# A four-layer graph network on one core: attention scores from 32-row matmuls, one head per row group and PSUM bank

## What is computed

```
h = relu(layernorm(x))                                   # [128, 128, 256]
q, k, v = split(h @ w_qkv)                               # 8 heads of 32
attn = einsum('bhnd,bhmd->bhnm', q, k) * 32 ** -0.5
attn = softmax(where(adj == 0, -inf, attn))
o = einsum('bhnm,bhmd->bhnd', attn, v) @ w_proj + b_proj
x = x + o + layernorm(o) * gamma + beta
# then three more layers: scores normalised by their norm; a graph attention
# with leaky ReLU and softmax; adj @ x @ weight + bias
```

## Time and profile before

| what | before |
|---|---|
| device time, median of 3 runs | 1971.55 us (1969.12 to 1973.96) |
| span of the profiled execution | 1971.0 us, 0.55 us under that median |
| PE busy | 1831.1 us, 93% |
| weight loads (PEld) busy | 1602.2 us, 81% |
| DVE busy | 1609.3 us, 82% |
| ACT busy | 1084.3 us, 55% |
| POOL busy | 674.6 us, 34% |
| chain that ended last, by engine | PE 48%, DVE 25%, issue 15%, POOL 9%, ACT 3% |

### The profile page before, as it was taken

The page is one execution under the profiler, slowest core; times in us unless marked ns, Lnnn a source line. Parts: engine busy times, 40 slices in busy tenths (PEclk is TensorE's granted clock), DMA queues, the critical chain, the costliest instruction groups (busy, mean ns, idle before and its releaser), DMA issues.

```text
span 1971.0 us, 39957 instructions
## 1 busy us (share of the span) xinstructions
PE 1831.1 (93%) x13064; PEld 1602.2 (81%) x13064; DVE 1609.3 (82%) x4485; ACT 1084.3 (55%) x2756; POOL 674.6 (34%) x1045
## 2 busy tenths in 40 slices
PE   6899999999999999999999999999999999999974
PEld 5788888878878888888878878788888878878864
DVE  3688897888888887887888888888887988978874
ACT  3555565655655555655655655655655655655632
POOL 3233333333333333333333333333332333333331
PEclk8999999999999999999999999999999999999987
DMA  2000000000000000000000000000000000000000
GB/s 88 12 17 17 23 23 11 21 16 16 21 17 16 22 16 17 21 16 16 22 16 16 21 17 16 22 16 16 22 16 16 22 16 16 21 16 17 12 6 17
DMA packets 37975, 37.85 MB, mean 19 GB/s; under 512 B 2416, under 2 KB 37488, under 8 KB 37872
## 3 DMA queue, kind: packets, MB, share of 16 engines
q1 hardware_dynamic: 37872, 36.84, 5.7%
HBM read 20.05 MB, written 16.78 MB: 19 GB/s over the span
## 4 chain that ended last, share of the span: by engine, by line
PE 48%; DVE 25%; issue 15%; POOL 9%; ACT 3%; DVEq 0%; POOLq 0%; DMA 0%; ACTq 0%
PE bank L314 15%; PE mid L387 11%; DVE stats L683 6%; DVE x L764 5%; PE bank L322 4%; POOL o_res L909 4%; POOL rstd L899 4%; PE bank L507 3%; PE mid L370 3%; PE bank L512 3%; PE bank L487 3%; DVE x L849 3%; DVE h_t_lo L699 2%; DVE o_gam L756 2%; ACT h_t_hi L559 2%
## 5 line engine op out<-in xcount | busy, mean ns | idle before, releaser
L567 ACT ACTIVATE probs<-mid,neg_max 128x128 f32<-128x128 f32 x1024 | 284.8, 379 | 105.2 <-DVE neg_max L713 105.2
L379 PE MATMUL mid<-k_diag,q_t 128*128 128x512 f32 x512 | 273.6, 617 | 0.0
L559 ACT ACTIVATE h_t_hi<-bank 128x512 fp32r<-128x512 f32 x192 | 114.9, 599 | 251.7 <-PE bank L322 251.6
L387 PEld LDWEIGHTS mid<-v,probs_t 128*128 128x128 f32 x2048 | 244.3, 192 | 3.3
L387 PE MATMUL mid<-v,probs_t 128*128 128x33 f32 x2048 | 239.9, 272 | 0.0
L899 POOL TENSOR_TENSOR rstd<-var_eps,minus_half 128x2 f32<-128x2 f32 x320 | 226.4, 707 | 25.1
L693 DVE TENSOR_SCALAR z<-x,mean_var,rstd 128x256 f32<-128x256 f32 x384 | 205.2, 575 | 10.8 <-POOL rstd L899 3.2
L713 DVE TENSOR_REDUCE neg_max<-mid 128x8 f32<-128x1024 f32 x128 | 154.6, 1208 | 51.1 <-issue 38.0
L897 POOL TENSOR_TENSOR var_eps<-mean_var,eps 128x2 f32<-128x2 f32 x320 | 66.0, 206 | 363.9 <-DVE mean_var L687 363.9
L322 PEld LDWEIGHTS bank<-ident,z 128*128 128x128 f32 x768 | 94.8, 152 | 112.4 <-DVE z L693 73.1
L322 PE MATMUL bank<-ident,z 128*128 128x128 f32 x768 | 125.8, 288 | 61.3 <-DVE z L693 61.3
(11 more groups left out here) (133 smaller groups left out, 5485.0 us busy)
## 6 DMA issues: line engine op xcount, KB each, us to landing
x<-in_x SPq DMA_DIRECT2D x64, 256.0 KB, 2.6
out_x<-x SPq DMA_DIRECT2D x64, 256.0 KB, 2.2
w_qkv_sb<-in_w_qkv SPq DMA_DIRECT2D x1, 768.0 KB, 4.8
w_q_sb<-in_w_q SPq DMA_DIRECT2D x1, 256.0 KB, 5.0
w_k_sb<-in_w_k SPq DMA_DIRECT2D x1, 256.0 KB, 5.3
w_proj_sb<-in_w_proj SPq DMA_DIRECT2D x1, 256.0 KB, 5.2
w_v_sb<-in_w_v_t SPq DMA_DIRECT2D x1, 256.0 KB, 5.4
w_gat_sb<-in_w_gat SPq DMA_DIRECT2D x1, 256.0 KB, 5.7
```

What stands on the lines that cost most here:

```text
L379: last = pe.matmul(mid[:, s], q_t[:, par, hc, b * N:(b + 1) * N], k_diag[:, hc, :, b * N:(b + 1) * N], start=False, stop=True)
L387: last = pe.matmul(mid[:, b, h * W33:(h + 1) * W33], probs_t[:, b * HC + h // RG, h % RG], v0[:, par, b, h], start=True, stop=True)
L559: act.activation(h_t[k][0][:], bank[:], ACT.Relu).then_inc(h_hi_ready[k], 1)
L567: last = act.activation(probs[:, s, r], mid[:, s, r * N:(r + 1) * N], ACT.Exp, bias=neg_max[:, s, r:r + 1])
```

## The change

The four heads of a chunk lie in q and k as projected in four groups of 32 rows. After the change each of the 16 blocks is a matmul of its own over 32 rows and 128 columns, with `tile_position=(r * 32, 0)`, so that it uses one row group of the array; the heads of row group r go to bank r of `mid`. `k_diag` becomes `k_t`, which one ACT copy of `bank6` fills; `keys_apart` is gone, on ACT and on DVE, and so is the fill of `k_diag` with zeros. `neg_max`, `probs` and `probs_t` are laid out by row group first. Both graphs' scores are made together, after q, the output projection and v, when all four banks are free. The order on ACT and DVE changes with that. A cut of the diff:

```diff
-        k_diag = sb("k_diag", [128, HC, RG, 2 * N])
+        k_t = sb("k_t", [128, HC, 2 * N])
...
@@ PE
-                def scores(b):
-
-                    for hc in range(HC):
-                        s = b * HC + hc
-                        pe.matmul(mid[:, s], ident_b[:], mask_b[:].unsqueeze(1).to_broadcast([128, RG, N]),
+                def scores():
+
                     for r in range(RG):
+                        pe.matmul(mid[:, r], ident_b[:], mask_b[:].unsqueeze(1).to_broadcast([128, BC, N]),
                                   start=True, stop=False)
-                        last = pe.matmul(mid[:, s], q_t[:, par, hc, b * N:(b + 1) * N],
-                                         k_diag[:, hc, :, b * N:(b + 1) * N], start=False, stop=True)
+                    for b in range(2):
+                        for hc in range(HC):
+                            s = b * HC + hc
+                            for r in range(RG):
+                                at = slice(r * HD, (r + 1) * HD)
+                                last = pe.matmul(mid[:, r, s * N:(s + 1) * N], q_t[at, par, hc, b * N:(b + 1) * N],
+                                                 k_t[at, hc, b * N:(b + 1) * N], start=False, stop=s == BC - 1,
+                                                 tile_position=(r * HD, 0))
                     last.then_inc(scores_psum, 1)
...
-                if middle:
-                    pe.wait_ge(q_ready, done(p2))
-                    pe.wait_ge(k_ready[0], done(p2))
-                    pe.wait_ge(k_ready[1], done(p2))
-                    wait_before(pe, o_heads_ready, p2, 2)
-                    scores(0)
...
                 if middle:
+                    pe.wait_ge(q_ready, done(p2))
+                    pe.wait_ge(k_ready, done(p2))
+                    wait_before(pe, o_heads_ready, p2, 2)
                     wait_before(pe, o_lo_ready, p2)
                     wait_before(pe, o_ready, p2)
-                    scores(1)
+                    scores()
...
-                if middle:
-                    transpose_probs(0)
...
-                if middle:
-                    transpose_probs(1)
                 if gat:
                     pe.wait_ge(h_hi_ready[2], done(p4))
                     pe.wait_ge(h_lo_ready[2], done(p4))
                     rows(bank4, h_t[2], w_gat_p, 0, hw_psum)
+                if middle:
+                    transpose_probs(0)
                 if front:
                     pe.wait_ge(v0_ready, done(p1))
                     columns(bank6, w_qkv_p, D, h_t[0], k_psum)
+                if middle:
+                    transpose_probs(1)
...
@@ ACT
                 if front:
-                    keys_apart(act, p1, 0)
+                    act.wait_ge(k_psum, done(p1))
+                    act.activation(k_t[:], bank6[:], ACT.Copy).then_inc(k_ready, 1)
...
@@ DVE
-                if middle:
-                    maxima(0)
                 if relation:
                     dve.wait_ge(o_psum, done(p3))
...
                     normalize(2, p4, z[2], x2[:, par], z_ready[2])
+                if middle:
+                    maxima(0)
...
                 if gat:
                     relu_lo(2, p4, bank4)
+                if middle:
+                    maxima(1)
                 if relation:
                     dve.wait_ge(x1_ready, done(p3, 2))
                     moments(1, p3, x1[:, 1 - par])
-                if middle:
-                    maxima(1)
...
-                if front:
-                    keys_apart(dve, p1, 1)
```

More of the change, by code:

```diff
@@ L184, in gnn_stack @@
         q_psum, k_psum, v0_psum = sem("q_psum"), sem("k_psum"), sem("v0_psum")
-        q_ready, k_ready, v0_ready = sem("q_ready"), [sem(f"k_ready{i}") for i in range(2)], sem("v0_ready")
+        q_ready, k_ready, v0_ready = sem("q_ready"), sem("k_ready"), sem("v0_ready")
         scores_psum, max_ready = sem("scores_psum"), sem("max_ready")
@@ L261, in gnn_stack @@
         SPLIT = [(w_proj_sb, w_proj_p), (w_v_sb, w_v_p), (w_gat_sb, w_gat_p), (w_out_sb, w_out_p)]
[L264 to L271, removed]
         @block.sync
@@ L381, in scores @@
                     last.then_inc(scores_psum, 1)
                 def heads_times_values(b):
-                    pe.wait_ge(probs_t_ready, done(p2, BC) - HC * (1 - b))
+                    if b == 0:
+                        pe.wait_ge(probs_t_ready, done(p2, RG))
                     for h in range(H):
-                        last = pe.matmul(mid[:, b, h * W33:(h + 1) * W33], probs_t[:, b * HC + h // RG, h % RG],
+                        last = pe.matmul(mid[:, b, h * W33:(h + 1) * W33], probs_t[:, h % RG, b * HC + h // RG],
@@ L559, in relu_hi, with exps, copy_probs_t @@
                     act.activation(h_t[k][0][:], bank[:], ACT.Relu).then_inc(h_hi_ready[k], 1)
[L561 to L568, removed]
+                def exps(r):
+                    if r % 2 == 0:
+                        act.wait_ge(max_ready, done(p2, 2) - (1 - r // 2))
+                    wait_before(act, probs_t_psum, p2, RG)
+                    for s in range(BC):
+                        last = act.activation(probs[:, r, s], mid[:, r, s * N:(s + 1) * N], ACT.Exp,
+                                              bias=neg_max[:, r, s:s + 1])
                     last.then_inc(probs_ready, 1)
-                def copy_probs_t(s):
-                    act.wait_ge(probs_t_psum, done(p2, BC) - (BC - 1 - s))
+                def copy_probs_t(r):
+                    act.wait_ge(probs_t_psum, done(p2, RG) - (RG - 1 - r))
                     wait_before(act, heads_psum, p2, 2)
-                    act.activation(probs_t[:, s], mid[:, s], ACT.Copy).then_inc(probs_t_ready, 1)
+                    act.activation(probs_t[:, r].rearrange("p s m -> p (s m)"), mid[:, r], ACT.Copy)\
+                       .then_inc(probs_t_ready, 1)
                 if front:
@@ L578, in step @@
                     act.activation(q_t[:, 1 - par], bank6[:], ACT.Copy, scale=SCALE).then_inc(q_ready, 1)
-                if middle:
-                    exps(0)
-                if middle:
-                    exps(1)
+                if front:
+                    act.wait_ge(v0_psum, done(p1))
+                    act.activation(v0[:, 1 - par, :, :, 0:HD], bank6[:].rearrange("p (b h d) -> p b h d", b=2, h=H),
+                                   ACT.Copy).then_inc(v0_ready, 1)
                 if last_layer:
@@ L591, in step @@
                     relu_hi(2, p4, bank4, [hw_psum])
-                if front:
-                    act.wait_ge(v0_psum, done(p1))
-                    act.activation(v0[:, 1 - par, :, :, 0:HD], bank6[:].rearrange("p (b h d) -> p b h d", b=2, h=H),
-                                   ACT.Copy).then_inc(v0_ready, 1)
+                if middle:
+                    exps(0)
                 if last_layer:
@@ L600, in step @@
                 if middle:
+                    exps(1)
+                if gat:
+                    act.wait_ge(hw_psum, done(p4))
+                    act.activation(hw[:], bank4[:], ACT.Copy).then_inc(hw_ready, 1)
+                if middle:
                     copy_probs_t(0)
@@ L603, in step @@
                     copy_probs_t(1)
-                if gat:
-                    act.wait_ge(hw_psum, done(p4))
-                    act.activation(hw[:], bank4[:], ACT.Copy).then_inc(hw_ready, 1)
                 if middle:
```

39 lines of the change are left out of this document (18 added, 21 removed).

## The result

The changed kernel takes 2228.64 us, median of four runs (2220.48 to 2236.22), against 1971.87 for the kernel before, also four runs: 1.1299 times as long, interval 1.1273 to 1.1324. That is 257 us more, where 112 were forecast. The sign is right, but the size is more than double. The time lies inside the range of 2025 to 2232 by luck: its upper end was set by the rival with a shared weight path, at 2228 us, and the trace refutes that rival. That both say 2228 is chance.

What follows compares the result with a forecast made beforehand. A step was taken as PE's 13.04 us plus 15.80 us set by DVE. 45 steps at 2.19 us and 14 loop turns at 0.94 us add 112 us to 1971.0: 2083 us, range 2025 to 2232.

Steps and rivals of the forecast that it cites:

- shared weight path: Rival for the score blocks on PE: row groups' weight loads do not overlap, S = 3.56 us; 257 us more, 2228 us; 12%.
- Which stretch bounds: Per step, PE's 13.04 us plus 15.80 us set by DVE; scores lie in DVE's stretch, so PE time saved there gains nothing.
- The walk of one step: Following one full step in the new order to `y_t_lo`: 1.09 us + S later, 2.19 us more with S = 1.1.
- S: Time from first to last start of the 16 score blocks on PE; taken as 1.1 us, row groups side by side.
- The estimate of 1.16 us: Alternative figure for the score blocks' first-to-last start time on PE: 3.56 us divided by the skill's measured 3.07x.
- The turn of the loop: At each of 14 hardware-loop turns DVE's 3.00 us stall covers the projection wait, so a turn costs 0.94 us more.
- PE is long done with v at a turn: At a loop turn, PE finishes v before DVE's stall ends, so masks can start once `o` is read, at 1024.95.
- The clock: Rival: PE's new idle gaps drop its granted clock to half for 4.32 us of products; at most 254 us more, 2330 us; 6%.
- Half overlap: Rival for the score blocks on PE: pairs side by side or issue-limited, S = 1.78 us; 152 us more, 2123 us; 13%.
- hidden S: Rival: the score blocks' time on PE hides behind DVE's work; 60 us more, 2031 us; 8%.
- PE as the bound: Rival: PE limits after all, so shorter scores save 2.34 us in 64 steps, 150 us off, 1822 us; 7%.
- The collision of `x3b`: Rival: POOL's `x3b` add no longer meets DVE's z(1), 1.54 us becoming near 0.8; 45 us off 2083, 2038 us; 4%.

Runs made afterwards that it cites:

- two_steps: The changed kernel with a hardware loop of 2 steps in place of 4, no fillers; four runs took 2135.33 to 2215.53 us, no ratio given.
- before_padded: The kernel before with 24 one-column matmuls, read by nobody, added per step where PE waits for z(1); 2003.69 us, ratio 1.0158.
- before_two_steps: The kernel before with a hardware loop of 2 steps in place of 4; 1937.54 us, ratio 0.9824.
- filler_two_steps: The changed kernel with 17 unread filler matmuls a step in PE's gaps and a hardware loop of 2 steps in place of 4; 2066.01 us, ratio 1.0475.
- experiment 4: The kernel before, keeping full-height scores and keys copied apart, with the changed kernel's order on PE, ACT and DVE; 2253.43 us, ratio 1.1407.
- filler: The changed kernel with 17 unread matmuls a step in PE's two gaps, loop of 4 steps; 2146.19 us, ratio 1.0877.
- experiment 3: The changed kernel with its 16 score blocks issued row group by row group, so neighbours share rows and bank; 2384.61 us, ratio 1.2091.
- own_bank: The changed kernel with a 2-step loop, six fillers, projection in bank 5 ahead of q, scores before v, DVE and ACT reordered; 1920.76 us, ratio 0.9734.

## Why the prediction was right or wrong

**The 257 us, by differences of medians.** The order: 2066.01 - 1937.54 = 128.5. The turns of the loop: (2146.19 - 2066.01) - (1971.87 - 1937.54) = 45.9. The clock: 2228.64 - 2146.19 = 82.4. These are paths through four kernels, so they close by construction, and another path would share out the sum otherwise: with the short body the clock costs 69 us in the quickest run of `two_steps`, and more in the others. What each contains is shown apart: the order's by steps of 30.95 against 28.85 us, 31 of the 45.9 by `before_padded`, the clock's by the granted clock. Some 10 of the other 15 us are no long body's: `before_two_steps` pays 0.4 us in every second step, which `filler_two_steps` does not. The last 5 are open: the fillers lengthen the body once more (q8 153 packets), and what that costs was not tried.

**Which stretch bounds: right.** The scores lie in DVE's stretch, and the time saved on them on PE came to nothing. DVE's and ACT's key copies were worth nothing either: DVE lost 137 us of work, but PE's stretch, from `y_t_lo` to the next `x2`, is 14.9 us at full clock and was 15.0.

**The walk of one step: right.** Forecast 2.19 us, found 2.17 in a step at full clock. Its terms: `o` 0.82 us after DVE is ready, forecast 0.8; 0.97 for the scores, forecast 1; 1.23 for POOL, forecast 1.2; the `x1` pair 0.88, forecast 0.90. S, from first to last start, was 0.90 us, forecast 1.1. What S lacks stands around it: ahead of the blocks the four masks take 0.97 us (995.59 to 996.56) instead of 0.88, and the maxima start 0.43 us behind the last block's start instead of 0.35. The three misses cancel, so part of the agreement is luck.

By the Trainium skill, "TensorEngine Tiling (Array Packing)", Key Properties, tiles load and multiply in parallel; this trace agrees, with 0.90 us against 2.55 group by group. The same section of the Trainium skill says that a change of the tiling mode drains TensorE; the 0.09 us more ahead of the blocks may be that, and nothing here tells it from other causes. The estimate of 1.16 us from the Trainium skill's "TensorE: Matmul & The Clock Gate" was too high: the 0.90 us are a quarter of 3.56, as four groups side by side would have it.

The 128.5 us of experiments 6 and 7 look like 59 steps at 2.17. In their traces a step costs 2.1 us more, and the stretch from the first `y_t_lo` to the last 114 us; the other 15 come ahead of the first `y_t_lo`, at 130.6 us instead of 115.6, where no cost was forecast.

**The turn of the loop: failed.** "PE is long done with v at a turn" was the step. PE with 24 more pairs in a step has a fetch stall of its own (3.87 us), q comes late by it, and DVE then waits 5.39 us for PE. That a stall of DVE can cover the wait for the projection was right in kind: in experiment 4 no turn is dearer. But DVE's stall was no fixed cost of the turn; it was a fetch too, gone in a body half as long. The turns were forecast at 0.94 us more each, 13 us in all. Measured where the clock is up, the 13 steps with a turn take 37.2 us on average in `filler` and 32.3 in the kernel before: 4.9 us more each, 63 us, of which the order would account for 2.1 each. (The body runs 14 times, with 13 jumps back.)

**The clock: failed, and the larger miss.** The sum has no term for the clock, because "a gap of 2.23 us at a turn left the granted clock at 1.00". That was read from one turn and taken as a rule. The trace of the kernel before has 13 such turns, with gaps of 2.0 to 2.4 us on PE, and behind 8 of them the granted clock fell. The very next one, with a gap of 2.08 us at 1144.50:

```profile
1144.00:1151.00 7.00, 6.50 (x30) 4.42 (x31) 6.04 (x17) 4.81 (x14) 3.58 (x4) 0.76 0.11 37
```

The turn steps with a fall take 32.3 to 32.9 us, those without 31.7 to 31.8. So the evidence lay in the trace of the kernel before, and gaps of this kind, 1.76 and 2.36 us, now came twice in every step. The mechanism stood among the rivals at 6%, with up to 254 us (2083 and 254 make 2337, not 2330); 82 were found. The loss has a second part, that the rival did not have: in a step at the low clock the exponentials come late too (the ACT rows in the chain above), and PE's own stretch is up to 16.3 us instead of 14.9.

**The rivals.** Shared weight path: refuted by S = 0.90 us and by experiment 3, though its number was met. Half overlap and hidden S: refuted by the 0.90 us and by the wait of 0.97. PE as the bound: refuted, DVE's three waits decide. It comes true in the layout of `own_bank`, where the shorter scores do count: with full-height scores there PE holds 77% of the chain, with the 32-row ones 47%. The collision of `x3b` did not go: the pair of z(1) still takes 1.61 us.

## What to carry to other kernels

Ask in which engine's stretch the saved work lies before counting it, and if an idle PE is the result, add the price of the clock, or fill the gap with matmuls that nobody reads: here 17 in a step gave 82 us back. Look at every occurrence of a gap in the trace before taking its clock as a rule; one of 13 was read here, and 8 said otherwise. Count the instructions of each engine in a hardware loop's body: a stall with no cause at its turn, with many packets on the engine's instruction queue, went away here with a shorter body. And when an order is forced by a shared PSUM bank, give one of the two a bank of its own before trading the order for a faster operation.

## What the hardware showed that was not expected

- Instruction fetch goes by the number of instructions in the loop's body, not by the work: q8 20 packets before, 139 with 24 short pairs more in each step, 13 with the body halved; q14 83 and 12. Halving the body alone was worth 34 us of 1972.
- The clock can change its pattern within one execution of one program: in `two_steps` a mean of 0.95 in one stretch and 0.88 in a later one. Its runs took 2135 to 2216 us, with a clock of 0.94 in the quickest and 0.89 in the slowest.
- The same gap can leave the clock up or not: behind gaps of 2.0 to 2.4 us at the turns of the kernel before it stayed at 1.00 in 5 cases and fell in 8.
- 32-row float32 instructions of one row group start 0.11 us apart, like full-height ones. Four row groups, each with its own bank, start theirs within 0.02 us of each other, so 32 instructions need 0.90 us from first to last start.
